# A graph network on one core: one more kept block, a simulated order of loads and adds, and a last diagonal block in halves

## The chip, the cores and the metric

One core of one Trainium2 chip runs the kernel. The metric is the device time of one execution in microseconds. TensorE (PE) multiplies, VectorE (DVE) and ScalarE (ACT) work elementwise, GpSimd (POOL) does small things, SyncE (SP) issues most DMAs. "us" is microseconds.

## The reference

`A` (`adj`) is 8192 x 8192 float32, `x` is 8192 x 128 float32. What is computed:

```
d  = rsqrt(sum(A, axis=1) + 1e-6)                    # degree of each row
y  = x + (d[:,None] * (A + I) * d[None,:]) @ (x @ W0)
x1 = layernorm(y)
agg = A @ x1
msg = relu(agg @ Wmsg.T + bmsg)
h  = gru_cell(msg, x1)                               # gates r, z, n from msg and x1
out = layernorm(x1 + h)
```

The first product needs the degrees, which need all of A; the second needs `x1`, which needs the whole first product. So A (268 MB) is read twice, but a part of the first product can be made while A is read for the degrees.

## The kernel before

**Blocks.** A is laid out in 8 x 8 panels of 1024 rows by 1024 columns, stored transposed. A unit (P, j) is row panel P with the 256 columns 256j to 256j+255: 1 MB, one DMA. There are 256 units (`T1`). A tile (i, k) of the second part is 512 x 512, also 1 MB, in two DMAs (`T2`, 256 tiles).

**First part.** Stage P (P from 0 to 7) loads the units left of row panel P's degrees. VectorE adds every unit into a sum (L650 to L664). When row panel P is through (`row_ends`), it folds the sum (L669), TensorE makes degrees from it (`degrees`, L341), GpSimd and ScalarE turn them into `dinv` and the scaled features (`feature`). With the features of panel Q, TensorE can multiply any unit whose columns lie in panel Q, exactly in float32: `product` (L356), four matmuls that leave two records each. The units below the diagonal are multiplied after their columns' features exist: in stage P those of columns 4P-4 to 4P-1 (`stage_products`), three of them (`LATE`) behind the degrees. The diagonal units (P, 4P..4P+3) are loaded before the features exist; they are kept in their slots and multiplied in `burst[P]`, behind the features. `BAND` lists row panels for which the four units right of the diagonal block are kept too, until the next panel's features: so far row panel 0 alone. All others above the diagonal are left to the second part.

**Slots.** 15 slots of 1 MB: `ring` (0 to 3), `kept` (4 to 11), `pool3` (12 to 14). Load n may be issued when the unit before it in its slot is summed and, if it takes part in a product, multiplied (`slot_free1`, waits in order on SP). The loop at L77 to L103 gives slots by a rough clock; the last eight loads go to slots 4 to 11. Products of one row panel and four column units form a group in two PSUM banks. Groups alternate between two pairs of banks; ScalarE moves the first eight out (`evict`), VectorE adds the others to `part` (`add_group`, L637), each behind the unit that `add_after` names. A group may begin when the group two before it has left (`group_left`).

**Second part.** A tile is split into `hi` (ScalarE, L544) and `lo` (VectorE, L682), and each layer takes 12 matmuls (L388 to L390). Tiles that had no product are read first, 108 of them (`N2`), and used for both layers: `layer0` with the features split in `f0`, `layer1` with x1. The other 148 are then used for `layer1` alone. Block rows (512 rows) whose first layer is complete are turned by TensorE (`turn`, L435), normalised on VectorE and split (`x1_hi`, `x1_lo`); `layer1` of a column block waits for that. Block rows 14 and 15 (`whole`) are complete with the first part, all others at the end of their row of tiles. The GRU of a block row is spread over the loop: step s of row i runs at n = `gru_at[i]` + s, at least 9 tiles apart (x1t 1, msg 3, gates 5 on TensorE; aggregate 3, blend 11 and output 16 on VectorE). All engines run the same loop over n in their own order.

At the change of parts TensorE does: all products of the last group, `layer0(0)`, the turns of 15 and 14, `layer0(1)`, `layer1(0)`. VectorE adds the last group whole before the turns.

## Time and profile before

| what | us |
|---|---|
| median of 3 runs | 1881.12 (1879.24 to 1881.31) |
| the profiled execution | 1881.41 |
| its span | 1879.6 |
| TensorE busy | 1704.1 (91%) |
| VectorE busy | 1445.6 (77%) |
| ScalarE busy | 644.8 (34%) |
| mean DMA rate | 293 GB/s, 551.10 MB |

The rest between span and time lies around the execution. The page cuts the span in 40 slices of 47 us: the first part fills some 15 of them, with DMA near full and VectorE at 9 tenths; then DMA is at half and TensorE at 9 tenths to the end. Busy shares are averages over parts with different limits, so the stage's own rows are read. Matmul records overlap: the time from one start to the next is the price, not the mean length.

### The profile page before, as it was taken

The numbers are of one execution on the slowest core, as the hardware profiler recorded it, in microseconds if no ns is written. First come the engines' busy times: TensorE is split into PE (matmuls) and PEld (weight loads), VectorE is DVE, ScalarE is ACT, GpSimd is POOL, SyncE is SP. The second block draws the span as 40 slices with busy tenths as digits, with TensorE's granted clock in tenths as the row PEclk, the third lists the DMA queues.
The fourth block names the chain that finished last, engine by engine and source line by source line (L and its number), as shares of the span: only waits on it lengthen the run. The fifth ranks groups of instructions, "written<-read, shape, count | busy, mean of one in ns | idle before, by whom it ended". The sixth has DMA issues, their size and how long they took to land.

```text
span 1879.6 us, 16726 instructions
## 1 busy us (share of the span) xinstructions
PE 1704.1 (91%) x6416; PEld 1166.7 (62%) x6416; DVE 1445.6 (77%) x1348; ACT 644.8 (34%) x564; POOL 115.8 (6%) x110
## 2 busy tenths in 40 slices
PE   0088799997989988999999999999999999999995
PEld 0043344443444445888888888888777777777773
DVE  7978899999999945776666656555778787888884
ACT  0000000000000012444444444444566565656561
POOL 0000000000000010200000000000001101010111
PEclk8589999999999999999999999999999999999997
DMA  9989999999999851666566666656899898989880
GB/s 392 422 359 422 421 421 422 421 421 421 421 416 422 334 206 63 204 197 202 193 204 191 199 192 198 198 189 197 320 339 309 289 319 291 310 292 309 301 287 17
DMA packets 180927, 551.10 MB, mean 293 GB/s; under 512 B 13424, under 2 KB 13936, under 8 KB 148080
## 3 DMA queue, kind: packets, MB, share of 16 engines
q1 hardware_dynamic: 177280, 541.11, 77.9%
q0 software_dynamic: 2560, 8.39, 1.3%
q8 instruction: 51, 0.84, 0.2%
q10 hardware_dynamic: 1008, 0.53, 0.1%
q14 instruction: 28, 0.23, 0.0%
HBM read 545.79 MB, written 4.19 MB: 293 GB/s over the span
## 4 chain that ended last, share of the span: by engine, by line
PE 63%; DVE 21%; DMA 11%; issue 4%; ACT 1%; SPq 0%; POOL 0%; DVEq 0%; ACTq 0%; POOLq 0%
PE bank L388 16%; PE bank L389 16%; PE bank L390 16%; DVE colsum L657 10%; DMA kept<-adj_blocks 7%; PE bank L356 6%; DMA ring<-adj_blocks 4%; DVE feat L661 4%; DVE feat L664 3%; DVE part L637 1%; PE bank L455 1%; PE bank L459 1%; PE bank L460 1%; PE bank L468 1%; PE bank L466 1%
## 5 line engine op out<-in xcount | busy, mean ns | idle before, releaser
L682 DVE TENSOR_TENSOR lo<-ring,hi 128x2048 fp32r<-128x2048 f32 x208 | 474.8, 2288 | 301.0 <-ACT f L550 225.3
L544 ACT ACTIVATE hi<-ring 128x2048 fp32r<-128x2048 f32 x208 | 398.8, 1918 | 398.6 <-DMA ring<-adj_blocks 255.9
L388 PE MATMUL bank<-hi,x1s 128*128 128x512 f32 x1024 | 416.8, 407 | 6.4 <-DVE x1s L732 4.1
L390 PE MATMUL bank<-hi,x1s 128*128 128x512 f32 x1024 | 399.5, 390 | 0.0
L356 PE MATMUL bank<-kept,feat 128*128 128x512 f32 x736 | 335.0, 607 | 33.9 <-DMA kept<-adj_blocks 23.6
L389 PE MATMUL bank<-lo,x1s 128*128 128x512 f32 x832 | 324.8, 390 | 0.0
L356 PEld LDWEIGHTS bank<-kept,feat 128*128 128x128 f32 x736 | 140.2, 194 | 218.3 <-issue 167.3
L657 DVE TENSOR_TENSOR colsum<-colsum,kept 128x2048 f32<-128x2048 f32 x103 | 236.0, 2291 | 32.2 <-DMA kept<-adj_blocks 30.4
L388 PEld LDWEIGHTS bank<-hi,x1s 128*128 128x128 f32 x1024 | 192.7, 188 | 56.6 <-DVE lo L682 6.7
L390 PEld LDWEIGHTS bank<-hi,x1s 128*128 128x128 f32 x1024 | 192.6, 188 | 41.5
L517 ACT ACTIVATE dege<-bank 128x8 f32<-128x8 f32 x8 | 1.4, 177 | 523.9 <-PE bank L341 523.9
L389 PEld LDWEIGHTS bank<-lo,x1s 128*128 128x128 f32 x832 | 156.8, 188 | 35.5 <-issue 5.3
L388 PE MATMUL bank<-hi,f 128*128 128x512 f32 x432 | 168.6, 390 | 0.0
L390 PE MATMUL bank<-hi,f 128*128 128x512 f32 x432 | 168.1, 389 | 0.0
L389 PE MATMUL bank<-lo,f 128*128 128x512 f32 x432 | 168.1, 389 | 0.0
L682 DVE TENSOR_TENSOR more_lo<-more,hi 128x2048 fp32r<-128x2048 f32 x48 | 109.4, 2283 | 20.8 <-ACT hi L544 20.8
L544 ACT ACTIVATE hi<-more 128x2048 fp32r<-128x2048 f32 x48 | 92.0, 1916 | 57.4 <-PE bank L390 52.7
L356 PE MATMUL bank<-pool,feat 128*128 128x512 f32 x232 | 106.0, 604 | 5.2 <-DMA pool<-adj_blocks 4.0
L356 PE MATMUL bank<-ring,feat 128*128 128x512 f32 x216 | 96.6, 594 | 2.3 <-DMA ring<-adj_blocks 2.0
L856 POOL TENSOR_TENSOR var<-mv,eps_ln 128x4 f32<-128x4 f32 x32 | 35.7, 1116 | 995.9 <-DVE mv L695 995.9
L388 PEld LDWEIGHTS bank<-hi,f 128*128 128x128 f32 x432 | 81.1, 188 | 17.1 <-issue 0.2
L389 PEld LDWEIGHTS bank<-lo,f 128*128 128x128 f32 x432 | 81.1, 188 | 17.0 <-issue 0.2
(96 smaller groups left out, 1540.3 us busy)
## 6 DMA issues: line engine op xcount, KB each, us to landing
ring<-adj_blocks SPq DMA_DIRECT2D x416, 512.0 KB, 5.2
kept<-adj_blocks SPq DMA_DIRECT2D x160, 1024.0 KB, 15.0
pool<-adj_blocks SPq DMA_DIRECT2D x49, 1024.0 KB, 16.7
more<-adj_blocks SPq DMA_DIRECT2D x96, 512.0 KB, 6.1
ring<-adj_blocks SPq DMA_DIRECT2D x47, 1024.0 KB, 15.2
xt<-x_t SPq DMA_DIRECT2D x8, 512.0 KB, 6.6
xin<-x POOLq DMA_DIRECT2D x16, 256.0 KB, 3.3
out<-y POOLq DMA_DIRECT2D x16, 256.0 KB, 4.0
```

Source lines behind the costliest of these rows:

```text
L356: mm = pe.matmul(bank[g % 2 * 2 + h][:, :], feat0[:, j * 2 + u, :], unit(slot_of1[n])[:, u, h * W:(h + 1) * W], start=begins and u == 0 an ...
L388: pe.matmul(acc[:, :], fh, ah, start=start and c == 0, stop=False, skip_group_check=True)
L389: pe.matmul(acc[:, :], fh, al, start=False, stop=False, skip_group_check=True)
L390: mm = pe.matmul(acc[:, :], fl, ah, start=False, stop=stop and c == KC - 1, skip_group_check=True)
L455: pe.matmul(p_x[:, :], wmsg_s[:, :], tall[:, :], start=True, stop=True).then_inc(msg_done, 1)
L459: pe.matmul(p_r[:, :], whh_s[:, 0:D], h, start=True, stop=False)
L544: ins = act.activation(hi[:, n % NHI], raw(slot_of2[n]), ACT.Copy)
L657: dve.tensor_tensor(cs, cs, slot(slot_of1[n]), ALU.add).then_inc(sum_done, 1)
L661: dve.tensor_tensor(row_sums(R), row_sums(R), of[:, 0, :], ALU.add).then_inc(fold_done, 1)
L664: dve.tensor_tensor(row_sums(R), row_sums(R), of[:, 1, :], ALU.add).then_inc(sum_done, 1)
L682: ins = dve.tensor_tensor(flat(low(n)), flat(raw(slot_of2[n])), flat(hi[:, n % NHI]).bitcast(f32), ALU.subtract)
L856: pool.tensor_tensor(var[:, at % 2], mv[:, at % 2, :, 1:2], eps_ln[:, :, :], ALU.add).then_inc(veps_ready, 1)
```

## The change

`BAND` gets row panel 2, so the units (2, 12..15) are loaded with the kept units of stage 2 and multiplied in `burst[3]`, behind the features of panel 3. The first-layer work of the four tiles that they cover leaves the second part (`N2` is 104). The clock at L77 is replaced by one that follows SP, TensorE and VectorE event by event, always taking the event with the earliest beginning; from it come slots, the place of each add and the place of each `x_t` load. The slots are renamed at the end, so that those that come free last are those needed last. The last diagonal block's products (units (7, 28..31)) are cut: the half for block 15 of all four first, then the half for block 14, and the turn of 15 in the middle of that. Each half has its own add. ScalarE's `split_hi` is cut in `hi_tile` and `hi_f0`, and x1_hi of 15 comes between them for tile 2.

```diff
@@ -23,7 +23,7 @@
 
 
     NP, NU, WP = N // 1024, 32, 1024
-    BAND = (0,)
+    BAND = (0, 2)
     LATE = 3
...
@@ -74,36 +74,113 @@
 
 
 
-    free = {s: 0.0 for s in range(15)}
-    held, count = {}, {s: 0 for s in range(15)}
-    slot_of1, before1, loads1 = [], [], []
-    come, pe_at = 0.0, 0.0
-    left_at = {}
+
+
+    LANDS, REUSE = 0.93, 0.6
+    SUM, SUM_LOW, SUM_FIRST, FOLD, ADD = 0.92, 1.0, 0.8, 0.5, 0.52
+    PRODUCT, SELF, DEGREES, SUPPORT, FEATURE, EVICT, MARGIN = 1.38, 0.72, 0.68, 0.72, 1.9, 0.56, 0.8
+    stage_first, stage_of = {}, []
     for P in range(NP):
-        for t in stage_units(P):
+        stage_first[P] = len(stage_of)
+        stage_of += [P] * len(stage_units(P))
+    xt_after = {stage_first[P] + len(stage_units(P)) // 2: P + 1 for P in range(NP - 1)}
+    xt_after[2] = 0
+    own_first = {P: min(n for n in range(NT1) if stage_of[n] == P and T1[n][0] == P) for P in range(NP)}
+    pe_work = [("support", 0)]
...
+        pe_work += [("product", t) for t in after_degrees[P]] + [("features", P)]
+        pe_work += [("support", P + 1)] * (P + 1 < NP) + [("product", t) for t in burst[P]]
+
+    landed, summed, multiplied, left, folded, featured, xt_there, supported = {}, {}, {}, {}, {}, {}, {}, {}
+    holder, slot_of1, before1, add_after, ended_groups = {}, [], [], {}, {}
+    now = {"sp": 0.8, "pe": 0.0, "dve": 0.0}
+    at_pe, at_sum, xt_next, to_fold = 0, 0, None, None
+    while at_pe < len(pe_work) or at_sum < NT1:
+        ready = []
+        if xt_next is not None:
+            if xt_next == 0 or xt_next - 1 in supported:
+                ready.append((max(now["sp"], supported.get(xt_next - 1, 0) + REUSE), 3, "xt", xt_next))
+        elif len(slot_of1) < NT1:
+            frees = []
+            for s in range(15):
+                m = holder.get(s)
+                if m is None:
+                    frees.append((0.0, s))
+                elif m in summed and (T1[m] in multiplied or not early_unit(*T1[m])):
+                    frees.append((max(summed[m], multiplied.get(T1[m], 0)) + REUSE, s))
+            if frees:
+                t, s = min(frees)
+                ready.append((max(now["sp"], t), 3, "load", s))
+        if at_pe < len(pe_work):
+            kind, of = pe_work[at_pe]
+            if kind == "product":
+                g = group_of[of]
+                needs = [landed.get(at1[of])] + [left.get(g - 2)] * (g >= 2 and groups[g][1][0] == of)
+            else:
+                needs = [{"support": xt_there, "degrees": folded, "features": featured}[kind].get(of)]
+            if None not in needs:
+                ready.append((max([now["pe"]] + needs), 2, kind, of))
+        if to_fold is not None:
+            ready.append((now["dve"], -1, "fold", to_fold))
+        elif at_sum in landed:
+            ready.append((max(now["dve"], landed[at_sum]), 1, "sum", at_sum))
+        ready += [(max(now["dve"], t), 0, "add", g) for g, t in ended_groups.items()]
+        begin, _, kind, of = min(ready)
+        at_pe += kind in ("product", "degrees", "features", "support")
+        if kind == "load":
             n = len(slot_of1)
-            slots = range(4, 12) if n >= NT1 - 8 else range(15)
-            s = min(slots, key=lambda s: free[s])
-            slot_of1.append(s)
-            before1.append(held.get(s))
-            count[s] += 1
-            loads1.append(count[s])
-            held[s] = n
-            come = max(come + 1, free[s] + 2.5)
-            if t in stage_products(P):
-                pe_at = max(pe_at, come + (8 if t in after_degrees[P] and t[0] == P else 0)) + 1.4
-                free[s] = pe_at
-                left_at[group_of[t]] = pe_at
-            else:
-                free[s] = 1e9 if kept_unit(*t) else come + 1
-        pe_at = max(pe_at, come + 3)
-        for t in burst[P]:
-            pe_at += 1.4
-            free[slot_of1[at1[t]]] = pe_at
-            left_at[group_of[t]] = pe_at
-
-
-    add_after = {g: min(NT1 - 1, max(int(left_at[g]) + 3, max(at1[t] for t in groups[g][1]))) for g in range(NP, len(groups))}
+            slot_of1.append(of)
+            before1.append(holder.get(of))
+            holder[of] = n
+            now["sp"] = begin + 1
+            landed[n] = now["sp"] + LANDS
+            xt_next = xt_after.get(n)
+        elif kind == "xt":
+            now["sp"] = begin + 0.5
+            xt_there[of] = now["sp"] + LANDS
+            xt_next = None
+        elif kind == "product":
+            now["pe"] = multiplied[of] = begin + PRODUCT + (SELF if of[1] == 4 * of[0] else 0)
+            g = group_of[of]
+            if groups[g][1][-1] == of:
+                if g < NP:
+                    left[g] = now["pe"] + EVICT
+                else:
+                    ended_groups[g] = now["pe"] + MARGIN
+        elif kind == "degrees":
+            now["pe"] = begin + DEGREES
+            featured[of] = now["pe"] + FEATURE
+        elif kind == "features":
+            now["pe"] = begin
+        elif kind == "support":
+            now["pe"] = supported[of] = begin + SUPPORT
+        elif kind == "sum":
+            P = stage_of[of]
+            now["dve"] = begin + (SUM_FIRST if of == own_first[P] else SUM if T1[of][0] == P else
+                                  SUM / 2 if T1[of][1] == 0 else SUM_LOW)
+            summed[of] = now["dve"]
+            at_sum += 1
+            if row_ends[T1[of][0]] == of:
+                to_fold = T1[of][0]
+        elif kind == "fold":
+            now["dve"] = folded[of] = begin + FOLD
+            to_fold = None
+        else:
+            now["dve"] = left[of] = begin + ADD
+            add_after[of] = at_sum - 1
+            del ended_groups[of]
+
+
+    freed_at = {s: max(summed[m], multiplied.get(T1[m], 0)) for s, m in holder.items()}
+    first_needed = [0, 12, 1, 13, 2, 14, 11, 3, 10, 9, 8, 7, 6, 5, 4]
+    place = dict(zip(sorted(freed_at, key=lambda s: freed_at[s]), first_needed))
+    slot_of1 = [place[s] for s in slot_of1]
+    held = {place[s]: n for s, n in holder.items()}
+    count, loads1 = {s: 0 for s in range(15)}, []
+    for s in slot_of1:
+        count[s] += 1
+        loads1.append(count[s])
 
 
...
+        def group_bank(g, h):
+
+            return bank[(g + len(groups)) % 2 * 2 + h]
+
         def low(n):
 
...
             for n, (P, j) in enumerate(T1):
                 if before1[n] is not None:
                     slot_free1(before1[n])
                 s = slot_of1[n]
                 sp.dma_start(unit(s), adj_blocks[P * NP + (P - j // 4) % NP, j % 4]).then_inc(slot_in[s], 16)
-                if n == 2:
-                    load_xt(0)
-                if n in xt_at:
-                    load_xt(xt_at[n])
+                if n in xt_after:
+                    load_xt(xt_after[n])
 
             for n, (i, k) in enumerate(T2):
                 s = slot_of2[n]
...
+            def half_product(P, j, h):
+
+                n, g = at1[(P, j)], group_of[(P, j)]
+                if h == 1:
+                    pe.wait_ge(slot_in[slot_of1[n]], loads1[n] * 16)
+                for u in range(2):
+                    mm = pe.matmul(group_bank(g, h)[:, :], feat0[:, j * 2 + u, :],
+                                   unit(slot_of1[n])[:, u, h * W:(h + 1) * W], start=False,
+                                   stop=j == 4 * P + 3 and u == 1, skip_group_check=True)
+                if h == 0:
+                    mm.then_inc(prod_done, 1)
+                elif j == 4 * P + 3:
+                    mm.then_inc(half_done, 1)
+
             for P in range(NP):
                 for R, j in before_degrees[P]:
                     product(R, j)
@@ -378,8 +471,14 @@
                 pe.wait_ge(feat0_ready, P + 1)
                 if P + 1 < NP:
                     support(P + 1)
-                for R, j in burst[P]:
-                    product(R, j)
+                    for R, j in burst[P]:
+                        product(R, j)
+            last = NP - 1
+            add_self(last, group_of[(last, 4 * last)], False)
+            for R, j in burst[last]:
+                half_product(R, j, 1)
+            for R, j in burst[last][:2]:
+                half_product(R, j, 0)
 
             def layer(n, stationary, acc, start, stop):
                 for c in range(KC):
...
-                    group_left(pe, len(groups) - 1)
+                    pe.wait_ge(last_added, q + 1)
                 else:
                     pe.wait_ge(tall_ready, rows2.index(i) + 1)
...
 
+            turn(whole[1])
+            for R, j in burst[last][2:]:
+                half_product(R, j, 0)
             layer0(0)
-            for i in whole[::-1][:2]:
-                turn(i)
+            turn(whole[0])
             layer0(1)
             layer1(0)
-            for i in whole[::-1][2:]:
-                turn(i)
             for n in range(1, NN + TAIL):
                 if 2 <= n < N2:
...
+            def hi_f0(n):
+                i, k = T2[n]
                 if n < N2:
                     if n == 0:
                         act.wait_ge(feat0_ready, NP)
...
-                x1_hi(i)
+            for n in range(2):
+                hi_tile(n)
+                hi_f0(n)
+            hi_tile(2)
+            x1_hi(whole[1])
+            hi_f0(2)
+            x1_hi(whole[0])
             for n in range(3, NN + TAIL):
                 if n < NN:
-                    split_hi(n)
+                    hi_tile(n)
+                    hi_f0(n)
                 i = normed_row(n, 3)
                 if i is not None:
...
-                    for g in range(NP, len(groups)):
+                    for g in range(NP, len(groups) - 1):
                         if add_after[g] == n and n < NT1 - 1:
                             add_group(g)
 
...
-            first = whole[::-1]
-            last_groups = [g for g in range(NP, len(groups)) if add_after[g] == NT1 - 1]
-            for g in last_groups[:-1]:
-                add_group(g)
+            def add_half(h):
+
+                g = len(groups) - 1
+                if h == 1:
+                    dve.wait_ge(half_done, 1)
+                else:
+                    dve.wait_ge(prod_done, len(products))
+                rows = part[:, (2 * groups[g][0] + h) * W:(2 * groups[g][0] + h + 1) * W]
+                dve.tensor_tensor(rows, rows, group_bank(g, h)[:, :], ALU.add).then_inc(last_added, 1)
+
+            for g in range(NP, len(groups) - 1):
+                if add_after[g] >= NT1 - 1:
+                    add_group(g)
             split_lo(0)
             split_lo(1)
-            add_group(last_groups[-1])
-            dve.wait_ge(added, len(groups) - NP)
-            row_step(first[0])
-            if len(first) > 1:
-                row_step(first[1])
-            x1_step(first[0])
-            x1_lo(first[0])
-            for a, b in zip(first[1:], first[2:]):
-                row_step(b)
-                x1_step(a)
-                x1_lo(a)
-            if len(first) > 1:
-                x1_step(first[-1])
-                x1_lo(first[-1])
+            add_half(1)
+            row_step(whole[1])
+            add_half(0)
+            x1_step(whole[1])
+            x1_lo(whole[1])
+            row_step(whole[0])
+            x1_step(whole[0])
+            x1_lo(whole[0])
             for n in range(2, NN + TAIL):
                 if n < NN:
                     split_lo(n)
```

The bank of a group is `group_bank(g, h)` wherever it was `bank[g % 2 * 2 + h]`.

## Rows read from the trace of the kernel before

**Rows 1.** Windows; columns: length, busy PE, PEld, DVE, ACT, POOL, granted clock, DMA share, GB/s.
```profile
158.00:232.00 74.00, 54.69 (x119) 21.51 (x120) 65.58 (x42) 4.34 (x8) 0.00 (x0) 1.00 1.01 422
...
354.00:458.00 104.00, 91.53 (x240) 41.77 (x240) 102.28 (x72) 2.35 (x9) 1.64 (x1) 0.98 1.01 422
458.00:724.00 266.00, 252.43 (x729) 125.70 (x729) 222.26 (x157) 18.17 (x50) 13.00 (x7) 0.96 0.83 336
...
741.00:1318.00 577.00, 575.31 (x2563) 475.78 (x2562) 362.43 (x444) 276.85 (x237) 31.90 (x38) 1.00 0.61 197
1318.00:1846.00 528.00, 525.09 (x2203) 397.37 (x2202) 424.87 (x419) 324.27 (x223) 54.68 (x44) 1.00 0.87 300
1846.00:1880.00 34.00, 13.10 (x36) 6.55 (x34) 12.90 (x35) 5.14 (x8) 4.02 (x6) 0.69 0.05 15
```

**Rows 2.** TensorE's timeline, waits in brackets: start, us, line, tiles.
```profile
276.07 3.70 PE L356 MATMUL bank<-pool,feat 128*128 128x512 f32 x8 [0.28 <-DVE part L637]
...
458.07 2.58 PE L341 MATMUL bank<-ones,y 128*128 128x1 f32 x16 [3.90 <-DVE y L669]
...
540.85 3.37 PE L341 MATMUL bank<-ones,y 128*128 128x1 f32 x16 [4.61 <-DVE y L669]
...
650.10 5.40 PE L356 MATMUL bank<-kept,feat 128*128 128x512 f32 x8 [2.23 <-DVE part L637]
...
691.30 5.38 PE L356 MATMUL bank<-kept,feat 128*128 128x512 f32 x8 [6.42 <-DVE part L637]
```

**Rows 3.** Chain of waits near 710: start, us, what.
```profile
708.76 1.78 PE bank L364 x16
710.55 13.73 PE bank L356 x32
```

**Rows 4.** TensorE's timeline, two layers of one tile.
```profile
1316.10 0.39 PE L388 MATMUL bank<-hi,f 128*128 128x512 f32 x1
...
1318.82 0.39 PE L388 MATMUL bank<-hi,x1s 128*128 128x512 f32 x1
```

**Rows 5.** Groups by line: the add of a group on VectorE.
```profile
L637 DVE TENSOR_TENSOR part<-part,bank 128x512 f32<-128x512 f32 x56 | 35.7, 680 | 13.7 <-PE bank L356 13.7
```

**Rows 6.** Timeline of the DMA queue's issues.
```profile
95.65 0.33 SPq L308 DMA_DIRECT2D ring<-adj_blocks  x1
112.05 0.33 SPq L308 DMA_DIRECT2D kept<-adj_blocks  x1
...
630.78 51.08 SPq L308 DMA_DIRECT2D kept<-adj_blocks  x8
```

**Rows 7.** VectorE's timeline: a sum, and the column sums of panel 3.
```profile
98.32 2.29 DVE L657 TENSOR_TENSOR colsum<-colsum,kept 128x2048 f32<-128x2048 f32 x1 [0.19 <-DMA kept<-adj_blocks]
...
456.79 1.23 DVE L669 TENSOR_TENSOR y<-colsum 128x1024 f32<-128x1024 f32 x1
```

**Rows 8.** Timeline at the change of part.
```profile
726.89 1.03 PE L435 MATMUL bank<-ident,part 128*128 128x128 f32 x8
...
727.60 1.13 DVE L718 SCALAR_TENSOR_TENSOR y<-bank,dinv,xin 128x128 f32<-128x128 f32 x4 [1.99 <-issue]
...
734.82 0.50 PE L388 MATMUL bank<-hi,x1s 128*128 128x512 f32 x1 [4.13 <-DVE x1s L732]
```

**Rows 9.** Chain of waits, at 739 and at the end.
```profile
739.45 0.54 SPq L291
...
1839.48 0.86 PE bank L455 x2
...
1847.38 0.87 PE bank L468 x2
...
1854.10 1.12 PE bank L476 x4
1855.21 1.71 PE bank L455 x2
```

**Rows 10.** The page's part 6: size and median us to landing.
```profile
kept<-adj_blocks SPq DMA_DIRECT2D x160, 1024.0 KB, 15.0
```

More of the change, by code:

```diff
@@ new lines, in gnn_resnorm_kernel @@
+    xt_after[2] = 0
+    own_first = {P: min(n for n in range(NT1) if stage_of[n] == P and T1[n][0] == P) for P in range(NP)}
+    pe_work = [("support", 0)]
+    for P in range(NP):
+        pe_work += [("product", t) for t in before_degrees[P]] + [("degrees", P)]
+        pe_work += [("product", t) for t in after_degrees[P]] + [("features", P)]
+        pe_work += [("support", P + 1)] * (P + 1 < NP) + [("product", t) for t in burst[P]]
+    landed, summed, multiplied, left, folded, featured, xt_there, supported = {}, {}, {}, {}, {}, {}, {}, {}
@@ L301, in slot_free1 @@
                     sp.wait_ge(prod_done, product_no[T1[m]])
-            xt_at = {at1[stage_units(P)[8]]: P + 1 for P in range(NP - 1)}
             for n, (P, j) in enumerate(T1):
```

26 lines of the change are left out of this document (12 added, 14 removed).

## The prediction

> **What bounds the kernel now.** I read the page first, then a table of windows by stage, then TensorE's waits, the DMA queue's issues and the chain of waits. The windows [rows 1] cut the run at the times at which the degree sums of panels 1, 2 and 3 are ready (232, 354, 458), at the last exact product (724) and at the change from tiles read for both layers to tiles read for the second alone (1318). The reader is to see three things.
> - Up to 458 three resources are close together: DMA is full at 421 GB/s from 158 on, VectorE is busy 102.3 of 104 us from 354 to 458, and TensorE has gaps.
> - From 458 to 724 TensorE is busy 252.4 of 266 us, so 13.6 us idle; DMA stands at 0.83. The gaps are few and named [rows 2]: 4.61 us for the column sums of panel 4, 2.23 and 6.42 us for a group's add on VectorE. After three of these gaps the next work ran at the clock's lower level (1.2 instead of 2.4 GHz): the degree matmuls took 3.37 us and two products 5.40 and 5.38 us.
> - From 741 to 1846 TensorE is busy 575.3 of 577 and 525.1 of 528 us. What takes matmuls out there shortens the run one for one. After 1846 it is busy 13.1 of 34 us: a serial tail.
>
> So the cost of this edit is TensorE time in the middle, and VectorE's time before 458.
>
> **Unit prices** [rows 3, 4]. Four products take 13.73 us in the chain, 3.43 each; adding the panel's own features 1.78. One layer of one 512x512 tile takes 2.72 us (1318.82 - 1316.10), 12 matmuls of 0.2267.
>
> **Part 1: the kept block, (2, 12..15).** Four 1024x256 units become products in the first part. They are the 512x512 tiles (4,6), (4,7), (5,6), (5,7), which now are read once in the second part for both layers. N2 goes from 108 to 104, the tiles of the last part from 148 to 152. Removed between 741 and 1318: 4 x 2.72 = 10.9 us of TensorE, and four f0 copies and subtractions on ScalarE and VectorE that were hidden anyway. Both stretches around 1318 are full on TensorE, so all 10.9 counts. **-10.9.**
>
> The Trainium skill (TensorE: Matmul & The Clock Gate, "Wait - 56ns, not 53.3ns?") gives 215.7 ns from start to start for 512 columns at the full clock. By it these 48 matmuls would be worth 10.4 us; the row shows 226.7 ns, and the row decides.
>
> Added in the first part: 4 x 3.43 = 13.7 us of products, between the degrees of panel 3 (458) and the first products of stage 4. Also one more group, hence one more add on VectorE, 2 x 0.68 = 1.3 us [rows 5], placed before the sums of panel 3 end.
>
> **Part 2: the order.** The new planner changes which slot each load takes, when adds come, and frees the last eight loads from the rule that they go to slots 4 to 11.
> - Start. Load 39 was issued at 95.65, load 40 at 112.05 [rows 6]: load 40 waited for the first product, load 41 took the slot of a unit that needs no product. The planner gives load 40 the slot of load 35, whose sum began at 98.32 and lasts 2.29 [rows 7], so it goes out at about 100.7. Load 41 still waits for 112. One load of 2.49 us (1.05 MB at 421 GB/s) is won of a longer pause; VectorE follows DMA closely there, so it carries to the sums. **-2.5, and +1.3 for the added add: panel 3's column sums about 1.2 us earlier than 456.79** [rows 7]. The ends are -6.5 (a full removal of the pause that follows) and 0.
> - Slots. Eight slots instead of four are kept from load 109 on: (2, 12..15) until 490. I followed which load waits for which: 110 for the product of (2,5), which ends at about 280 (the first product of stage 2 began at 276.07 [rows 2], and 3.43 each), 112 for (2,7) at 287, 114 for (3,5) at 294, 117 at 301. DMA at full rate brings load 112 at about 298 and 117 at 311, so these are a few us before they are late. Then VectorE paces: at 2.6 us a load (104 us for 40, from 354 to 458) seven slots give 18 us a round, and DMA needs 2.5 plus a few. So panel 3's sums hold. After 458 loads 184, 186, 187, 189 wait for the four new products (from 476 on, 3.43 apart), with loads without a product between them: 17 loads in 36 us, faster than DMA.
> - TensorE from 458 on. Products 89 to 92 are new. They push all that follows back by 13.7; this eats first what was idle. Idle 13.6, and the slow clock 1.6 + 1.8 + 1.8 = 5.2. The wait of 4.61 goes because TensorE now comes later than the sums (540.85 + 13.7 - 4.6). The two waits for adds go because adds come 4 to 6 loads earlier. The last eight loads, issued over 51 us from 630.78 [rows 6], lose their cause; VectorE has 44 us of idle time in this stretch (266 - 222.3 [rows 1]), nearly all behind those late loads; without them its last column sums come well before TensorE wants them (about 690: the end at 718, less the seven products behind the degrees, 24.0, the features added, 1.8, and the degree matmuls themselves, 1.8). TensorE is never idle from 458 to the end of the products: from 458.07 [rows 2] to 724.28 (710.55 + 13.73, [rows 3]) are 266.2 us; 266.2 - 13.6 - 5.2 + 13.7 = 261.1, 5.1 less, and 1.2 for the earlier start. **-6.3.** Last product at about 718.
>
> **Part 3: halves and the change of stage.** The same matmuls in another order. Before: last product, first-layer tile 0, two turns, tile 1, then 4.13 us waiting for x1 (734.82), and the slow clock for the 12 matmuls that follow: SP's wait for them ends at 739.45, 4.6 us instead of 2.72 [rows 8, 9]. After: the columns of block 15 are complete after four half products; it is added and turned while four half products (2 x 3.43 = 6.9 us for four units, half of it behind the turn) remain. From the first normalising instruction (727.60) to the start of the matmul that needs x1 (734.82) are 7.2 us. TensorE has 3.4 + 2.7 + 0.5 (a turn; two took 1.03) + 2.7 = 9.3 us of its own between turn and need: no wait. Block 14 is turned 6.6 us after block 15, so its x1 is there at 13.8, and TensorE wants it at 12.0: a wait of up to 1.8, nothing of it before. I take 1.5. 4.1 + 1.9 - 1.5: **-4.5.** (Bounds: -6, and -2.5 if the wait lowers the clock again.)
>
> **Part 4: the tail.** The GRU steps come every 9 tiles from the end of the first row on; this row ends 4 tiles earlier while the tiles still end at 255. The last GRU begins at 256 instead of 260, and the gates of the one before it come before tile 253 instead of behind tile 255. Before [rows 9]: last tile done at 1845.66, three gate matmuls (2.59 us, the last ends 1848.25), then sigmoid, multiply, tanh and blend, and the last row's aggregate queued behind them on VectorE: message matmul at 1855.21, at the lower clock (1.71 for what took 0.86 at 1839.48). After: the three last tiles (8.2 us) cover that chain (5.9 us from 1848.25 to 1854.10), and the message matmul follows the last tile after 1.4 us of transposes. 9.55 - 2.6 - 1.4 = 5.5, and two matmul pairs at full clock, 1.7. **-7.2.** (Bounds: -5 to -8.)
>
> **Sum.** -10.9 - 6.3 - 4.5 - 7.2 = -28.9. The profiled execution took 1881.41 (span 1879.6), so 1852.5; the median of the runs is 1881.12, only 0.3 lower, and I leave it at 1852.5.
>
> The Trainium skill (TensorE: Matmul & The Clock Gate, "HAM oscillation") says that waits for data put TensorE back to its low clock and the work behind them pays. The gaps of 2 to 6 us above with 5.40 for 3.43 us agree; the 1.5 us wait I leave at block 14 would by it be cheap, and no row of before shows a gap of just that size.
>
> **Rivals.**
> - Slots starve (0.14). With eight kept, seven slots work. If a load keeps the 15.0 us from issue to landing that the page shows for these loads [rows 10], plus 2.29 for the sum, and for half of them 3.43 for a product, a round is up to 20.7 us, 2.96 a load against 2.6. Over loads 110 to 135 and 154 to 175 that is 17 us later at 458 (48 x 0.36): 1852.5 + 17 = 1869.5. Against it: stage 1 runs now with seven slots, and its window (158 to 232) shows DMA at 1.01 [rows 1]; the 15 us are the queue ahead of a load.
> - The other side, slower: adds too early (0.03). VectorE works in order and sets the sums until 458; 13 adds come before them, 4 to 5 loads earlier than now. If a group isn't finished at its add, VectorE waits up to one product each time, 13 x 3.43 = 44.6: 1897. It decides from 2.2 us an add on (28.9 over 13). Against it: by the walk above group (3, 4..7) ends at 301 and its add comes at about 306, the next at 315 and 322.
> - The products cost nothing (0.08): TensorE's gaps before 458 (19.3 us from 158 to 232 and 12.5 from 354 to 458 [rows 1]) are used too, since the planner lets arrivals come earlier. Then 13.7 disappears: 1839. Against it: the new products need features that exist only after 458.
> - The change does only half of what it says at its ends (0.05): a new late piece (block 14, or output of the row before) keeps tail and transition as they are: 1852.5 + 4.5 + 7.2 = 1864.
>
> **Chances.** My forecast 0.70, its own range 1847 to 1858. Range 1845 to 1865: it takes in the bounds of the pause (4 us), of the transition (3) and the tail (2), and a good part of the starved case. A difference of 0.2% (3.8 us) is what measurement can tell from nothing. Faster 0.95, same 0.02, slower 0.03: three of the four terms are matmuls or waits that fall away on a full engine, and only a loss of 26 us in the first part undoes them.
>
> **What the new profile would show.** L356 1216 matmul records instead of 1184, and 416 instead of 432 of the first layer at each of three lines. TensorE with no gap over 1 us from the degrees of panel 3 to 717. Loads 248 to 255 issued before 665. The first second-layer matmul about 6 us behind the last product instead of 11. About 8 us less between the last tile and the end. Wrong would be: column sums of panel 3 after 462 (slots), VectorE waiting for PE at the adds, or TensorE idle behind the new products.

## The result, and the profile after

| | us | ratio to before, 95% |
|---|---|---|
| before | 1880.65 (1879.24 to 1881.31, 4 runs) | |
| changed | 1847.57 (1845.82 to 1849.16, 4 runs) | 0.9825 [0.9808, 0.9842] |
| predicted | 1852.5, range 1845 to 1865 | |

The change takes 33.1 us off the median. The profiled execution of the changed kernel was the fastest of its four (1845.82, span 1844.0); against the profiled one of before the span is 35.6 us shorter, and the sums below are made on these two.

Windows of the changed kernel at its own milestones, columns as in [rows 1]: the end of stage 1, stage 2, stage 3 (which ends with panel 3's column sums), the stretch from panel 3's degrees to the last product, the tiles for both layers, the tiles for the second, the tail.

```profile
158.00:232.00 74.00, 58.04 (x134) 24.12 (x133) 64.17 (x42) 4.52 (x9) 0.18 (x1) 0.95 1.01 421
232.00:354.00 122.00, 117.74 (x308) 54.03 (x307) 118.44 (x82) 3.43 (x11) 3.22 (x2) 1.00 1.01 421
354.00:455.00 101.00, 88.12 (x222) 39.24 (x220) 99.32 (x70) 2.17 (x8) 0.35 (x1) 0.98 1.01 419
455.00:714.00 259.00, 259.00 (x766) 129.88 (x767) 225.34 (x170) 18.17 (x50) 13.20 (x9) 0.99 0.85 347
730.00:1280.00 550.00, 550.00 (x2452) 455.53 (x2451) 347.76 (x434) 265.70 (x227) 31.91 (x38) 1.00 0.61 197
1280.00:1819.00 539.00, 536.49 (x2250) 406.49 (x2249) 437.01 (x428) 332.50 (x229) 56.65 (x44) 1.00 0.87 301
1819.00:1844.00 25.00, 9.21 (x33) 4.82 (x31) 9.48 (x30) 3.27 (x5) 4.02 (x6) 0.73 0.07 21
```

The stretch after panel 3's degrees is 259 us long and TensorE is busy in all of it; before, 266 with 13.6 idle [rows 1]. The second part is as full as it was. The tail is 25 us instead of 34.

TensorE's timeline, the rows that answer to [rows 2] and [rows 8]: waits in brackets.

```profile
413.34 8.83 PE L435 MATMUL bank<-ring,feat 128*128 128x512 f32 x16 [2.29 <-DMA ring<-adj_blocks]
...
454.90 3.57 PE L420 MATMUL bank<-ones,y 128*128 128x1 f32 x16 [3.02 <-DVE y L775]
...
723.54 0.50 PE L487 MATMUL bank<-hi,x1s 128*128 128x512 f32 x1 [1.01 <-DVE x1s L838]
...
729.74 0.66 PE L534 MATMUL bank<-ident,tall 128*128 128x128 f32 x4 [0.37 <-DVE tall L816]
```

Behind 454.90 no wait follows until 723.54. The waits for adds at 650.10 and 691.30 and the one for panel 4's column sums at 540.85 [rows 2] are gone. The one before panel 3's degrees stays (3.02), and its matmuls take 3.57: the clock's low level.

VectorE's column sums of panels 1, 2, 3 and 7, and the DMA queue's issues (answering to [rows 6, 7]):

```profile
226.00 1.23 DVE L775 TENSOR_TENSOR y<-colsum 128x1024 f32<-128x1024 f32 x1
...
349.20 1.23 DVE L775 TENSOR_TENSOR y<-colsum 128x1024 f32<-128x1024 f32 x1
...
453.62 1.22 DVE L775 TENSOR_TENSOR y<-colsum 128x1024 f32<-128x1024 f32 x1
...
673.69 1.23 DVE L775 TENSOR_TENSOR y<-colsum 128x1024 f32<-128x1024 f32 x1
...
100.82 11.14 SPq L389 DMA_DIRECT2D ring<-adj_blocks  x2
112.00 0.43 SPq L389 DMA_DIRECT2D kept<-adj_blocks  x1
...
632.84 20.55 SPq L389 DMA_DIRECT2D kept<-adj_blocks  x7
```

Panel 3's sums begin 3.17 us earlier. Load 40 goes out at 100.82, where the prediction had 100.7. The last loads go out over 20.6 us from 632.84 instead of over 51.

The change of parts, TensorE's and VectorE's timelines (the half add, the turn of 15, the last products, tile 0 of the first layer, tile 0 of the second):

```profile
706.59 0.69 DVE L896 TENSOR_TENSOR part<-part,bank 128x512 f32<-128x512 f32 x1 [6.87 <-PE bank L457]
...
709.82 0.60 PE L534 MATMUL bank<-ident,part 128*128 128x128 f32 x4
...
710.26 3.60 PE L457 MATMUL bank<-kept,feat 128*128 128x512 f32 x8
...
713.29 0.79 PE L487 MATMUL bank<-hi,f 128*128 128x512 f32 x1
...
719.64 0.39 PE L487 MATMUL bank<-hi,x1s 128*128 128x512 f32 x1
```

The second layer's first matmul begins 6.35 us behind the first layer's (719.64 - 713.29); before 11.1 (723.72 to 734.82).

The tail in the chain of waits, answering to [rows 9]: message matmul of the row before, last gate matmul of it, message matmul of the last row, its turn.

```profile
1799.88 0.86 PE bank L554 x2
...
1810.50 0.86 PE bank L567 x2
...
1821.16 1.10 PE bank L554 x2
...
1833.27 1.13 PE bank L575 x4
```

The last gate matmul of the row before stands ahead of the last tiles, and the message matmul of the last row follows the last tile (whose last matmul begins at 1819.15) at the full clock.

### The profile page after: what moved, and what is told of

The parts are those of the page before. It is cut to its first block, busy times and chain, and to the rows that moved or that the text cites. A ratio compares the mean times of both kernels' runs of the same rounds, so it can differ in the third digit from the quotient of the medians.

```text
span 1844.0 us, 16697 instructions
## 1 busy us (share of the span) xinstructions
PE 1696.3 (92%) x6400; PEld 1160.4 (63%) x6400; DVE 1444.7 (78%) x1346; ACT 641.9 (35%) x560; POOL 117.0 (6%) x110
## 4 chain that ended last, share of the span: by engine, by line
PE 76%; DVE 12%; DMA 9%; issue 2%; ACT 1%; POOL 0%; SPq 0%; DVEq 0%; ACTq 0%; POOLq 0%
PE bank L487 17%; PE bank L489 17%; PE bank L488 17%; PE bank L435 15%; DMA ring<-adj_blocks 6%; DVE colsum L763 5%; DVE feat L767 2%; DVE feat L770 2%; DMA pool<-adj_blocks 2%; DMA kept<-adj_blocks 1%; PE bank L420 1%; PE bank L554 1%; PE bank L567 1%; PE bank L565 1%; PE bank L457 1%
## 5 line engine op out<-in xcount | busy, mean ns | idle before, releaser
L435 PE MATMUL bank<-kept,feat 128*128 128x512 f32 x600 | 267.9, 597 | 11.6 <-DMA kept<-adj_blocks 11.6
L435 PEld LDWEIGHTS bank<-kept,feat 128*128 128x128 f32 x600 | 113.2, 191 | 155.4 <-issue 137.5
L763 DVE TENSOR_TENSOR colsum<-colsum,kept 128x2048 f32<-128x2048 f32 x81 | 185.6, 2291 | 9.9 <-DMA kept<-adj_blocks 8.2
L435 PE MATMUL bank<-ring,feat 128*128 128x512 f32 x376 | 173.9, 610 | 16.0 <-DMA ring<-adj_blocks 16.0
L487 PE MATMUL bank<-hi,f 128*128 128x512 f32 x416 | 162.5, 391 | 0.0
L489 PE MATMUL bank<-hi,f 128*128 128x512 f32 x416 | 162.0, 389 | 0.0
L488 PE MATMUL bank<-lo,f 128*128 128x512 f32 x416 | 161.9, 389 | 0.0
L435 PEld LDWEIGHTS bank<-ring,feat 128*128 128x128 f32 x376 | 72.1, 195 | 110.3 <-issue 91.4
L763 DVE TENSOR_TENSOR colsum<-colsum,ring 128x2048 f32<-128x2048 f32 x50 | 114.5, 2291 | 16.4 <-DMA ring<-adj_blocks 15.6
L435 PE MATMUL bank<-pool,feat 128*128 128x512 f32 x208 | 93.7, 594 | 2.5 <-DMA pool<-adj_blocks 2.5
```

Of the source, the lines that this page charges most:

```text
L435: mm = pe.matmul(group_bank(g, h)[:, :], feat0[:, j * 2 + u, :], unit(slot_of1[n])[:, u, h * W:(h + 1) * W], start=begins and u == 0 and j ...
L487: pe.matmul(acc[:, :], fh, ah, start=start and c == 0, stop=False, skip_group_check=True)
L488: pe.matmul(acc[:, :], fh, al, start=False, stop=False, skip_group_check=True)
L489: mm = pe.matmul(acc[:, :], fl, ah, start=False, stop=stop and c == KC - 1, skip_group_check=True)
L763: dve.tensor_tensor(cs, cs, slot(slot_of1[n]), ALU.add).then_inc(sum_done, 1)
```

## The experiments

Eleven further kernels ran, each beside the kernel before; times are medians of four executions, and differences are between medians if nothing else is said. "Last product" is the start of the first matmul of `layer0(0)`, which follows it: 723.72 before, 713.29 after. Rows and starts come from one execution of each kernel. Where code is the same they still differ: up to the second part the kernel before and the one with GRU steps 8 apart do the same, and their last products are at 723.72 and 720.93.

### The block alone taken back

```diff
-    BAND = (0, 2)
+    BAND = (0,)
```

> The changed kernel with BAND = (0,): new planner and halves, without the new kept block. Theory (the terms add): 10.9 us come back in the second part (4 tiles x 2.72) and about 7 in the tail (9.4 less the 2.6 of the gate matmuls); in the first part 13.7 us of products go, but TensorE then comes to panel 4's degrees before their column sums (538 in the changed kernel, TensorE there at 546 - 13.7 = 532) and pays a wait of about 6 and a slow clock of about 3.5. Last product at about 710 instead of 713.9, total about 1861. Rival (the kept block holds slots and costs loads): the last product comes before 705 and the total is 1855 or less.

Measured: 1862.29 (0.9903 [0.9888, 0.9917]), last product at 710.18. So the block is worth 14.7 us on top of the rest. That fits 17.8 of the second part and the tail (10.9 and 6.9, the prices below), less 3.1 by which the first part grows. TensorE's wait has come back, with the slow clock:

```profile
539.06 3.58 PE L420 MATMUL bank<-ones,y 128*128 128x1 f32 x16 [5.83 <-DVE y L775]
```

The wait is the theory's (5.83 for about 6), and the degree matmuls behind it take 3.58, as behind the same wait before (3.37). Of 13.7 us of products, 10.6 go where TensorE waited or ran slowly.

### The last diagonal block whole

```diff
-            for R, j in burst[last][:2]:
+            for R, j in burst[last]:
                 half_product(R, j, 0)
...
-            turn(whole[1])
-            for R, j in burst[last][2:]:
-                half_product(R, j, 0)
             layer0(0)
+            turn(whole[1])
             turn(whole[0])
```

> The changed kernel with the last diagonal block whole again: all half products, then layer0(0), both turns, layer0(1); both adds after the last product. Theory: the wait of 4.1 us for x1 and the slow clock of about 1.9 behind it come back, the 1.0 + 0.4 us of waits at block 14 go: about +4.8, 1852.4, and everything up to the last product at 713.9 unchanged. Rival (the halves gain nothing that the next wait doesn't take): within 1.5 us of the changed kernel.

Measured: 1853.70 (0.9856 [0.9842, 0.9871]), 6.1 more than the changed kernel where 4.8 were expected. The wait for x1 is the old one, at the old length, with the low clock behind it (0.80 for the first matmul; 0.50 behind the wait of 1.01 in the changed kernel), and the last product is 0.6 later. The added 1.3 are not tied to one row: the waits for `lo` near 1300 also differ from execution to execution, see the end.

```profile
713.93 0.79 PE L487 MATMUL bank<-hi,f 128*128 128x512 f32 x1
...
724.93 0.80 PE L487 MATMUL bank<-hi,x1s 128*128 128x512 f32 x1 [4.09 <-DVE x1s L836]
```

### The block alone, on the kernel before

```diff
-    BAND = (0,)
+    BAND = (0, 2)
...
-    bank[g % 2 * 2 + h]
+    bank[(g + 1) % 2 * 2 + h]
```

> The kernel before with BAND = (0, 2) alone (banks of the groups swapped, since there are now 37). Theory: -10.9 in the second part, -7 in the tail; in the first part +13.7, of which the wait of 4.6 for the column sums of panel 4 and the slow clock of about 3.5 behind it are saved, while the waits for adds and the late last eight loads stay: last product at about 730, total about 1880.7 - 17.9 + 5.6 = 1868. Rival (the old slots cannot carry eight kept ones): DMA share under 0.95 between 354 and 500 and a total above 1875.

Measured: 1866.32 (0.9926 [0.9909, 0.9943]), last product at 725.44 instead of the 730 that I expected. The direction holds. The block costs the first part less than 5.6 us: 1.7 against the profile of before, 4.5 against the other profile of the same code (720.93). The wait at 540.85 is gone, the one at 650.10 too, which I had not counted on; a new one for an add stands at 488, and the big one before the last stage stays:

```profile
488.00 3.53 PE L364 MATMUL bank<-ident,feat 128*128 128x128 f32 x16 [2.49 <-DVE part L637]
...
692.94 5.46 PE L356 MATMUL bank<-kept,feat 128*128 128x512 f32 x8 [6.47 <-DVE part L637]
```

So TensorE coming later seems to hide waits for adds as well as waits for sums. The block gives 14.4 us on the old order and 14.7 on the new one: order and block add up.

This kernel and the one with the last block whole differ in the order of loads and adds, and beside it only in how the last adds and one of ScalarE's splits are written: both have the block, and neither has the halves. So the order by itself is 1866.32 - 1853.70 = 12.6 us. It lies in the first part: the last product is at 713.93 instead of 725.44 (11.5), panel 3's column sums at 453.24 instead of 456.36, and the waits of 2.49 and 6.47 shown above are gone. Waits for x1 (4.13 and 4.09) and tails (24.5) are the same.

### Half a block more

```diff
-        return j // 4 == P or (P in BAND and j // 4 == P + 1)
+        return j // 4 == P or (P in BAND and j // 4 == P + 1) or (P == 1 and j in (8, 9))
...
-    burst = {P: ([(P - 1, j) for j in range(4 * P, 4 * P + 4)] if P - 1 in BAND else []) +
+    burst = {P: [(P - 1, j) for j in range(4 * P, 4 * P + 4) if P and kept_unit(P - 1, j)] +
```

> The changed kernel with two more units kept, (1, 8) and (1, 9): tiles (2,4) and (3,4) leave the first layer of the second part (N2 = 102), ten slots are held in stages 1 and 2, five work. Theory: -5.4 in the second part; the two products (6.9 us) fall on TensorE's gaps between 354 and 455 (12.9 us idle), so column sums of panel 3 stay at 453.6 and the last product at 713.9: total about 1842. Rival (slots starve): with five working slots DMA falls below 0.95 between 158 and 354 and the column sums of panel 3 come 3 us or more later: total 1845 or above.

Measured: 1842.03 (0.9796 [0.9781, 0.9810]), 5.5 less than the changed kernel in the median; it is the fastest kernel here by median. Its windows show what each theory looks at:

```profile
158.00:232.00 74.00, 57.15 (x135) 23.79 (x134) 64.62 (x42) 4.52 (x9) 0.02 (x1) 0.98 1.01 421
232.00:354.00 122.00, 114.82 (x288) 51.31 (x287) 115.56 (x80) 3.26 (x10) 2.03 (x1) 1.00 1.00 407
354.00:455.00 101.00, 93.22 (x250) 42.73 (x248) 99.32 (x71) 2.35 (x9) 2.08 (x1) 1.00 1.00 410
...
456.62 1.23 DVE L775 TENSOR_TENSOR y<-colsum 128x1024 f32<-128x1024 f32 x1
```

DMA falls to 407 GB/s between 232 and 354 (421 in the changed kernel) and panel 3's sums come 3.0 us later, as the rival says. So the total is the theory's, but not by its step, which had the sums unmoved. The changed kernel waits 3.02 us for these sums and then runs at the low clock; here TensorE, with two products more, comes as late as the sums, there is no such wait and no slow clock, and the last product is at 713.89, 0.6 later. Ten held slots are felt, and a wait that was there anyway hides it.

### A block where TensorE has no gap

```diff
-    BAND = (0, 2)
+    BAND = (0, 2, 4)
```

> The changed kernel with BAND = (0, 2, 4): the block right of panel 4's diagonal is kept too, N2 = 100. Theory (TensorE is the bound from 455 on): 13.7 us of products more with no gap left to take them, 10.9 less in the second part: +2.8, about 1850.4, last product at about 727.6. Rival (the first part is still bound by VectorE or DMA, the products are hidden): last product within 5 us of 713.9, total about 1840. Second rival (slots starve): total above 1856.

Measured: 1851.44 (0.9848 [0.9831, 0.9864]), 3.9 more than the changed kernel; last product at 727.75, 14.5 later. The products are paid in full here, and by these numbers 10.6 come back (10.9 in the theory). TensorE is the bound from 455 on: the same 13.7 us of work cost 3.1 in `burst[3]` and 14.5 in `burst[5]`.

### The adds four units later

```diff
-            add_after[of] = at_sum - 1
+            add_after[of] = at_sum - 1 + 4
```

> The changed kernel with each add of a group four units later on VectorE, about where it stood before. Theory (the waits for adds went because the last eight loads come earlier, so VectorE is ahead of TensorE in the last stages): within 1.5 us of the changed kernel; gaps under 1 us at the first products of groups. Rival (the adds' places removed them): gaps of 2 to 6 us before products in 600 to 700 and a slow clock behind them, +8 or more.

Measured: 1846.67 (0.9822 [0.9807, 0.9836]), the same as the changed kernel, last product at 711.29. Between 455 and the last product the longest wait is 1.22 us, for an add at 512.92, and the clock stays full. So the adds' places in the planner did not remove the waits of [rows 2]. That leaves that VectorE is no longer behind late loads when an add is due; this is the theory, and no run puts the late loads back alone.

### The GRU steps at least 8 tiles apart, in the kernel before

```diff
-        g = max(end3[i], g + 9)
+        g = max(end3[i], g + 8)
```

> The kernel before with GRU steps at least 8 tiles apart instead of 9: the last GRU begins at tile 255 instead of 260. Theory (the tail's gain is only the place of the last GRU against the last tile): the end comes about 7 us earlier, 1874, all of it behind the last tile; message matmul about 1.5 us behind the last tile at the full clock. Rival (the tail's gain came from fewer tiles read for both layers): within 2 us of the kernel before.

Measured: 1872.37 (0.9962 [0.9947, 0.9977]). The profile's span is 9.1 us shorter, of which 2.8 are there before the second part (734.82 against 732.02 at the same matmul), so 6.3 in the tail. The 2.8 can't come from this edit, which acts in the second part. The message matmul of the last row, in the chain:

```profile
1836.36 0.86 PE bank L468 x2
...
1847.02 1.10 PE bank L455 x2
```

It runs at the full clock (1.10 with its wait, 1.71 before). The place of the last GRU alone brings 6.3 of the tail's 6.9 us, by a change of one digit in the kernel before.

### Load 40 as before

```diff
+            if len(slot_of1) == 40:
+                frees = [f for f in frees if holder[f[1]] == 24]
             if frees:
```

> The changed kernel, but load 40 must take the slot of load 24, as before, so it waits for the first product at 112; load 41 follows at once. All other choices are the planner's. Theory (the start pause of DMA carries one for one to all column sums): column sums of panels 1, 2, 3 about 2.5 us later than in the changed kernel (228.5, 351.7, 456.1), last product 2.5 later, total about 1850. Rival (the earlier column sums come from the other slots and the adds' places in stages 1 and 2): column sums of panel 1 at 226 as in the changed kernel, total within 1 us of 1847.6.

Measured: 1849.68 (0.9835 [0.9820, 0.9850]), 2.1 more; column sums of panels 1, 2, 3 at 228.53, 351.71 and 456.14, each 2.5 later. One execution differs from another by as much as 1.9 us in these sums, so the right pair has to be compared: where TensorE's first product starts at the same time, 108.03, panel 1's sums are at 226.04 (the kernel with later adds) and 228.53 (this one). The theory holds: one load's 2.5 us at 112 goes through all stages.

```profile
228.53 1.23 DVE L777 TENSOR_TENSOR y<-colsum 128x1024 f32<-128x1024 f32 x1
...
456.14 1.22 DVE L777 TENSOR_TENSOR y<-colsum 128x1024 f32<-128x1024 f32 x1
```

### The whole block of panel 1

```diff
-    BAND = (0, 2)
+    BAND = (0, 1, 2)
```

> The changed kernel with BAND = (0, 1, 2): all four units right of panel 1's diagonal are kept, N2 = 100; twelve slots are held in the second half of stages 1 and 2, three work. Theory (seven and five slots are enough, three are not: a load needs 2.5 us of DMA, some 2 to land, 2.3 for the sum and 3.4 for a product, so about 10 us a round, 3.4 a load instead of 2.6, over some 40 loads): column sums of panel 3 some 30 us later than 453.6, and with 10.9 us less in the second part the total is 1860 to 1870. Rival (slots don't bind, only TensorE does): as the half block, twice: about 1838 to 1842.

Measured: 1893.62 (1.0066 [1.0045, 1.0087]), slower than the kernel before. I expected 1860 to 1870.

```profile
158.00:232.00 74.00, 53.31 (x104) 21.56 (x104) 50.39 (x33) 3.26 (x6) 0.00 (x0) 0.91 0.85 327
232.00:354.00 122.00, 105.05 (x263) 48.05 (x264) 97.10 (x66) 4.52 (x13) 2.23 (x1) 0.94 0.89 345
354.00:455.00 101.00, 89.04 (x232) 40.78 (x231) 82.46 (x59) 2.35 (x9) 2.42 (x1) 0.97 0.89 344
...
509.23 1.23 DVE L775 TENSOR_TENSOR y<-colsum 128x1024 f32<-128x1024 f32 x1
```

Panel 3's sums are 55.6 us later than in the changed kernel, not 30. With three working slots DMA moves 327 to 345 GB/s over almost 300 us, where I had counted 40 loads. This is the prediction's rival of starved slots, at twelve held slots.

### Kept units loaded later

```diff
-        cut = min(len(body), 14 if P else 24)
+        cut = min(len(body), 24 if P < 3 else 14)
```

> The kernel with (1, 8) and (1, 9) kept, and the kept units of stages 1 and 2 loaded ten places later (cut 24 instead of 14), so that they hold their slots for a shorter time. Theory (its column sums of panels 2 and 3 came 3.0 us late because ten held slots slow the loads): DMA back at 421 GB/s between 232 and 354, column sums of panel 3 at 453.6, total 1839 to 1840. Rival (the 3.0 us don't come from held slots): same as with cut 14, 1842.

Measured: 1842.59 (0.9802 [0.9783, 0.9820]), four runs from 1839.69 to 1847.80. Panel 3's sums are at 455.66, one us earlier than with cut 14, but panel 1's are already 0.8 earlier (225.37 against 226.17). From one to the other it is 230.3 us, against 230.5 with cut 14 and 227.6 in the changed kernel: loading later wins next to nothing of the 3.0 back. DMA moves 414 GB/s from 232 to 354 and 408 behind it, so the slots still show. The total is not told apart from 1842.03.

### Three parts together

```diff
-        g = max(end3[i], g + 9)
+        g = max(end3[i], g + 8)
...
-            add_after[of] = at_sum - 1
+            add_after[of] = at_sum - 1 + 4
```

(on the kernel with half a block more)

> The kernel with (1, 8) and (1, 9) kept, GRU steps at least 8 tiles apart, adds four units later. Each part by the runs so far: the tail cannot shrink further, since the last GRU begins at tile 255 instead of 255 or 256 (0 to -0.5), the adds 0 to -1. Theory: 1841, not distinguishable from 1842. Rival (GRU steps closer together crowd VectorE in the last part, busy about 8 tenths there): TensorE waits for lo there, total above 1844.

Measured: 1852.66 (0.9852 [0.9837, 0.9867]), 10.6 more than the half block alone, and neither theory: the last part is no worse, the loss lies before 455.

```profile
354.00:455.00 101.00, 91.37 (x239) 42.80 (x237) 92.75 (x65) 2.35 (x9) 1.64 (x1) 0.97 0.92 375
...
382.42 3.78 PE L443 MATMUL bank<-ident,feat 128*128 128x128 f32 x16 [4.71 <-DVE part L743]
...
466.57 1.23 DVE L775 TENSOR_TENSOR y<-colsum 128x1024 f32<-128x1024 f32 x1
```

TensorE waits 4.71 us for an add at 382; it is then in the burst that frees the kept slots, so loads wait (DMA at 375 GB/s; the DMA queue's longest wait for a product is 12.6 us, 4.8 in the half block), and panel 3's sums come 10 us later than in the half block. Of these, 3.2 are there before that wait: panel 2's sums are at 355.42 instead of 352.19. The GRU steps cannot act there, so it is the late adds. They were free with seven working slots and are not with five.

## Why the prediction was right, and where its sizes were off

| step | predicted | profile |
|---|---|---|
| first part, to the last product | -6.3 | -10.4 |
| of it: panel 3's column sums | -1.2 | -3.2 |
| of it: 458 to 724 | -5.1 | -7.3 |
| change of parts | -4.5 | -4.8, then -1.9 for the clock and +1.4 for new waits |
| second part, 4 x 2.72 | -10.9 | -10.9 |
| tail | -7.2 | -6.9 |
| other small waits in the second part | 0 | -2.1 |
| sum | -28.9 | about -35.6 |

The last column is worked out so (parts are rounded). First part: 723.72 - 713.29. Change: 11.10 - 6.35. From the second layer's first matmul to the last tile the kernel before takes 1110.7 us (734.82 to 1845.50), the changed one 1099.7 (719.64 to 1819.38; both ends are the last matmul's start and 0.23): 10.9 less (from the unrounded times). It is made up of the 10.9 of tiles, 2.6 more for the gate matmuls that moved in, 1.9 less for the slow clock, and 0.7 less in small waits (1.4 new ones and 2.1 fewer others). The tiles' 10.9 is the price times four here, and the parts close on it. Tail: 34.1 - 24.6 = 9.5, less the 2.6.

The mechanism was right in all four parts, but for one term in panel 3's column sums. The forecast fell 4.2 us short in the medians, and the table says where: mostly in the first part.

- **Second part, halves, tail: right,** in mechanism and within a microsecond or so. The halves by the profiles: 4.8 and 1.9 less, 1.4 more for waits at block 14 (1.01 and 0.37, where I took 1.5; the clock stayed high), and 0.5 more for the turn of block 15 that now stands before the last product: 4.8 against 4.5. The run with the last block whole gives 6.1. The one with GRU steps 8 apart shows the tail's term by itself. By the Trainium skill (TensorE: Matmul & The Clock Gate, "Wait - 56ns, not 53.3ns?") an estimate for the tiles is 10.4 instead of 10.9. A half microsecond can't be read from the sum of the two traces, but the changed kernel's own rows show 2.72 us a layer again, 226.7 ns a matmul (TensorE's timeline, the first matmul of a second layer and of the first layer behind it):

```profile
1000.68 0.39 PE L487 MATMUL bank<-hi,x1s 128*128 128x512 f32 x1
...
1003.40 0.39 PE L487 MATMUL bank<-hi,f 128*128 128x512 f32 x1
```

- **"TensorE is never idle from 458 to the end of the products": right,** 259.0 of 259. The term was mis-sized (5.1 predicted, 7.3 measured) by what the slow clock costs: I counted it on the two degree matmuls and products that carried a wait. The product behind a slow degree matmul is slow too. These are the first products behind panel 3's and panel 4's degrees in the kernel before (TensorE's timeline):

```profile
460.51 6.41 PE L356 MATMUL bank<-kept,feat 128*128 128x512 f32 x8
...
544.08 5.59 PE L356 MATMUL bank<-pool,feat 128*128 128x512 f32 x8
```

  They have 3.60 at the full clock. The first stays in the changed kernel, behind the wait that stays; the second goes: 266.2 - 13.6 - 5.2 - 2.0 + 13.7 = 259.1, and 259.0 were measured (454.90 to about 713.9). The turn of block 15, 0.5, is in the measured one and not in the sum.
- **"Panel 3's column sums about 1.2 us earlier": mis-sized, and with a wrong term in it.** The load at 112 gave 2.5 as predicted (the run with load 40 as before). The 1.3 us set against it were for the add of the new block's group, "placed before the sums of panel 3 end". That can't be: its products stand behind panel 3's degrees. An add did come in front of these sums, but by the planner's order: without the block it is there as well. VectorE's groups of instructions from 100 to just before panel 3's sums, before, changed, and changed without the block:

```profile
L637 DVE TENSOR_TENSOR part<-part,bank 128x512 f32<-128x512 f32 x24 | 15.3, 680 | 0.0
```

```profile
L743 DVE TENSOR_TENSOR part<-part,bank 128x512 f32<-128x512 f32 x26 | 16.6, 679 | 0.0
```

```profile
L743 DVE TENSOR_TENSOR part<-part,bank 128x512 f32<-128x512 f32 x26 | 16.6, 680 | 0.0
```

  (an add of a group is two instructions). From panel 1's sums to panel 3's it is 228.0 us before, 227.6 in the changed kernel, and 226.7 in the run with adds four units later, which has 24 again. So that add costs about 0.9, and the rest of the new order wins about 1.2 there, which the prediction hadn't counted. The remaining 2.8 of the 3.2 lie before panel 1's sums: the load, and about 0.4 because this execution's first product started earlier (see the end).
- **The rival of starved slots** was false at eight held slots: 421 GB/s through stage 2, 419 in stage 3. It begins to show at ten and rules at twelve. **Adds too early** was false: before panel 3's sums VectorE is idle in front of no add (0.0 in the rows above). Behind them it waits for a group twice, 1.5 us at 470.5 and 7.4 at 682.4, where TensorE is the bound and VectorE's waiting costs nothing. **Products for nothing** was false: the gaps before 458 took none of them. What hid 10.6 of the 13.7 us was nearly all at panel 4's degrees: a wait, 5.83 us without the block, and the slow clock around it. The prediction's sum knew this place, with 4.6 and 1.6.

The parts by experiment, each between two kernels that differ in it and in little else: the block 14.4 (on the old order) or 14.7, the order 12.6, the halves 6.1. They make up the 33.1. Of the order 2.1 to 2.5 is load 40. The rest should be the last eight loads, issued over 20.6 instead of 51 us, and the waits for adds of 2.2 and 6.4 with their slow clock, which the adds' places did not remove. That split is argued, not run.

## What to carry to other kernels

Before adding work to an engine, sum its waits and the slow-clock work behind them in the very stretch where the work lands: here 13.7 us of products cost 3.1 in one place and 14.5 in another. A pool of held buffers gives way slowly and then fast: with eight of fifteen held DMA kept 421 GB/s; with ten it fell to 407, hidden by a wait that was there anyway, but adds four units late then cost 10 us; twelve cost more than the whole edit brings. And look where a fixed spacing lets the last dependent step fall against the end of the main work: one digit was worth 6 to 8 us (6.3 in the profile's tail, 7.9 between medians).

## What the runs showed of the hardware

- In the kernel before, the low clock behind a wait of 2.2 to 6.4 us costs another 1.8 to 3.6 us: 5.40 and 5.38 us for a product of 3.60 (waits of 2.23 and 6.42), or degree matmuls and the product behind them (1.6 and 2.0, wait of 4.61). Behind waits of about 2 us the clock went either way. TensorE's timeline of the changed kernel and of the half block:

```profile
191.27 5.40 PE L435 MATMUL bank<-ring,feat 128*128 128x512 f32 x8 [2.05 <-DMA ring<-adj_blocks]
```

```profile
184.16 3.70 PE L435 MATMUL bank<-kept,feat 128*128 128x512 f32 x8 [2.10 <-DMA kept<-adj_blocks]
```

  The first product, behind 2.05 us, runs at the low level (5.40), the other, behind 2.10, at the full one (3.70). A term for the clock behind such a gap has both ends.
- TensorE waits 66 us for the first degrees and then works at the low clock. When the clock rises differs between executions, and it moves all that follows. TensorE's first self-feature matmuls, a block of work of equal size, in the kernel before and in the one with GRU steps 8 apart, which is the same program up to there:

```profile
105.62 2.91 PE L364 MATMUL bank<-ident,feat 128*128 128x128 f32 x16
```

```profile
105.21 1.95 PE L364 MATMUL bank<-ident,feat 128*128 128x128 f32 x16
```

  The granted clock from 105 to 110 is 0.74 in the first and 1.00 in the second. The first product starts at 108.36 and 107.00, and as the next loads wait for it, panel 1's column sums start at 228.81 and 227.48. In the eight profiles with the new order, load 40 early and at most ten slots held, the first product starts between 107.25 and 108.78 and these sums between 224.91 and 226.79, the later the one, the later the other. A difference of a microsecond between two profiles is read only after this start has been taken off.
- The wait for `lo` where the tiles for both layers end also differs between executions: 0.99 us in the changed kernel, 2.19 with the last block whole, 3.15 with later adds, the last two with the clock at the low level around it. The changed kernel and the one with later adds have the same second part, and from its first second-layer matmul to the last tile they take 1099.7 and 1102.3 us, so two profiles are compared there with some 2.5 us of doubt.
